# A joined three-stage kernel: rotary embedding by swapped partitions, and six layers' inverse roots taken by a power on GpSimd

## The reference

```python
# stage A: layernorm + scale/shift, self-attention, cross-attention, gated feed-forward (16 heads of 64)
# stage B:
def _rope(x, theta):                       # pairs (even, odd) of a head's 64 dimensions are turned
    x1, x2 = (x[..., 0::2], x[..., 1::2])
    return concatenate([x1 * cos - x2 * sin, x1 * sin + x2 * cos], axis=-1)
xn = _rmsnorm(x, gamma1)
q, k = _rope(xn @ q_w + q_b), _rope(xn @ k_w + k_b)
attn = softmax(where(causal, q @ k.T / 8, -inf))          # 16 heads of 64
...                                                       # 31 routed experts, top 3
# stage C: six layers, each with three norms
def _ln(x, eps=1e-05):
    m = mean(x); v = var(x)
    return (x - m) * rsqrt(v + eps)
x = x + self_attention(_ln(x) ...); x = x + cross_attention(_ln(x) ...); x = x + feed_forward(_ln(x) ...)
# behind it a last stage of 64 experts
```

## Time and profile before

| what | us |
|---|---|
| median of 3 runs (lowest, highest) | 2443.45 (2440.22, 2444.05) |
| the profiled execution, its own time | 2436.98 |
| its span in the profile | 2435.4 |
| PE busy | 2093.1 (86%) |
| DVE busy | 1613.7 (66%) |
| ACT busy | 1247.7 (51%) |
| POOL busy | 140.8 (6%) |
| stage A's self-attention | about 18 to 300 |
| stage B's self-attention | about 454 to 709 |
| the layers of stage C | about 780 to 2263 |

### The profile page before, as it was taken

How to read it: one execution, slowest core, us unless ns; L and a number is a source line. 1 busy time by engine, 2 the same in 40 slices (tenths; PEclk the granted TensorE clock), 3 DMA queues, 4 the chain that set the end, 5 groups by cost and what they waited for, 6 DMA issues and landing times.

```text
span 2435.4 us, 32516 instructions
## 1 busy us (share of the span) xinstructions
PE 2093.1 (86%) x11008; PEld 917.6 (38%) x11008; DVE 1613.7 (66%) x4148; ACT 1247.7 (51%) x2398; POOL 140.8 (6%) x130
## 2 busy tenths in 40 slices
PE   7999988899999988778878887988788788868998
PEld 3444455545556522322232223322232322233433
DVE  6766576666757787467746756684677467653564
ACT  4565544355543346646645663666366546635311
POOL 0000000111120200000000000000000000010000
PEclk9999999899999989979997997999799979989999
DMA  4000000300010100001000100010010001030000
GB/s 156 1 1 1 1 1 1 122 1 1 1 55 3 46 1 27 1 27 45 1 25 3 46 1 27 3 44 1 27 45 2 5 23 27 5 104 1 1 1 9
DMA packets 38037, 54.36 MB, mean 22 GB/s; under 512 B 5073, under 2 KB 34546, under 8 KB 36338
## 3 DMA queue, kind: packets, MB, share of 16 engines
q1 hardware_dynamic: 37874, 52.28, 6.8%
HBM read 32.34 MB, written 0.52 MB: 13 GB/s over the span
## 4 chain that ended last, share of the span: by engine, by line
PE 40%; DVE 10%; ACT 9%; issue 4%; SPq 1%; DMA 0%; ACTq 0%; POOL 0%; DVEq 0%; POOLq 0%
PE ps L1938 7%; PE ps L1918 5%; ACT big L2418 4%; PE ps L1899 4%; DVE C_nm L2595 4%; PE ps L2066 3%; PE ps L1983 3%; PE ps L2173 2%; PE ps L2078 2%; ACT big L2498 2%; PE ps L2169 2%; PE ps L2194 2%; PE ps L2085 2%; PE ps L2094 2%; PE ps L2043 1%
## 5 line engine op out<-in xcount | busy, mean ns | idle before, releaser
L2595 DVE TENSOR_REDUCE C_nm<-ps 128x1 f32<-128x512 f32 x768 | 501.4, 685 | 178.0 <-PE ps L1899 173.7
L2418 ACT ACTIVATE big<-ps 128x512 f32<-128x512 f32 x768 | 427.9, 595 | 226.7 <-PE ps L1918 216.0
L1899 PE MATMUL ps<-C_attn 62*128 62x512 bf16 x768 | 274.5, 415 | 60.8 <-DVE C_nm L2595 51.6
L1918 PE MATMUL ps<-C_attn 64*128 64x512 bf16 x768 | 251.3, 393 | 63.2 <-ACT big L2418 52.7
L1938 PE MATMUL ps<-big,C_attn 128*32 128x512 f32 x1536 | 210.6, 621 | 13.3 <-ACT big L2418 13.3
L1899 PEld LDWEIGHTS ps<-C_attn 62*128 62x128 bf16 x768 | 63.1, 94 | 302.3 <-DVE C_nm L2595 165.9
L1918 PEld LDWEIGHTS ps<-C_attn 64*128 64x128 bf16 x768 | 59.3, 93 | 272.7 <-ACT big L2418 205.2
L2498 ACT ACTIVATE big<-ps,C_biasx 77x512 f32<-77x512 f32 x192 | 115.6, 679 | 57.8 <-PE ps L2070 57.7
L790 DVE TENSOR_REDUCE A_nm<-ps 128x2 f32<-128x1024 f32 x64 | 78.4, 1225 | 58.8 <-PE ps L618 58.5
L2557 ACT ACTIVATE big<-ps 128x512 f32<-128x512 f32 (+1 forms) x66 | 39.4, 597 | 149.0 <-PE ps L2169 146.7
L717 ACT ACTIVATE A_pT<-ps 128x512 f32<-128x512 f32 x128 | 69.9, 599 | 77.1 <-PE ps L634 77.1
(11 more groups left out here) (364 smaller groups left out, 3733.4 us busy)
## 6 DMA issues: line engine op xcount, KB each, us to landing
C_attn<-C_first SPq DMA_DIRECT2D x144, 128.0 KB, 2.4
C_w<-in_C_w SPq DMA_DIRECT2D x6, 1090.0 KB, 5.0
C_attn<-in_D_ew SPq DMA_DIRECT2D x4, 1536.0 KB, 10.5
big<-in_B_ew SPq DMA_DIRECT2D x8, 514.0 KB
normw_later<-in_norm_w SPq DMA_DIRECT2D x1, 2304.0 KB, 16.4
A_w<-in_A_w SPq DMA_DIRECT2D x2, 1024.0 KB, 11.8
A_w<-in_A_w SPq DMA_DIRECT2D x2, 768.0 KB, 8.8
B_w<-in_B_w SPq DMA_DIRECT2D x1, 1536.0 KB, 10.1
```

The costliest lines, as they stand in the source:

```text
L1899: pe.matmul(ps[:, bank, :], lhsT=qs[side(hp, MAX_ROW), b, 2 * q + pq, t * P:(t + 1) * P], rhs=ks[side(hp, MAX_ROW), b, 2 * q + pq, :], sta ...
L1918: pe.matmul(ps[:, bank, :], lhsT=ks[side(1 - hp, HALF), b, 2 * q + pq, kt * P:(kt + 1) * P], rhs=qs[side(1 - hp, HALF), b, 2 * q + pq, :], ...
L2418: act.activation(prob[:, kt % 2, pq, 1 - hp, :], ps[:, bank, :], ACT.Exp, scale=SCALE)\
L2595: dve.tensor_reduce(nm[:, q % 2, t, pq, hp:hp + 1], ps[:, bank, :], AX.X, ALU.max, negate=True).then_inc(emptied[bank], 1)
```

## The change

Three things change. (1) In stage B the swapped projections "qr" and "kr" are no longer computed. The weights stay in the reference's order of dimensions. ACT copies q and k with their bias from PSUM into `B_rot[:, i, 0]`; SP swaps neighbouring partitions by two DMAs of 64 rows of 2 KB into `B_rot[:, i, 1]`; DVE multiplies the first by cos into `B_q` or `B_k`; POOL multiplies the second by sin, and then adds it to DVE's product. (2) In `self_attention_block`, for stages A and B both, `add_out` moves ahead of the step's other work on DVE. (3) In stage C the twelve-instruction root leaves DVE. At the same slots POOL adds eps and raises to the power -0.5; DVE's APPLY waits for it.

```diff
-    pieces = ("q", "qr", "k", "kr") if causal else ("q", "k")
-    column = {"q": WQ, "qr": WQR, "k": WK, "kr": WKR}
-    at_step = (("q", "qr"), ("k", "kr"), ("v",), ()) if causal else (("q",), ("k",), ("v",), ())
+    column = {"q": WQ, "k": WK}
...
@@ POOL, stage B
-                            pool.wait_ge(roped, n * 4 + 2 * i + 2)
-                            if n >= 3:
-                                pool.wait_ge(s_done, (n - 2) * TB)
-                            pool.tensor_tensor(dst[:, n % 3, :], rot[:, i, 0, :], rot[:, i, 1, :], ALU.add)\
+                            turned_rows = rot[:, i, 1, :]
+                            pool.wait_ge(swapped[i], 32 * (n + 1))
+                            pool.tensor_tensor(turned_rows, turned_rows, rope[i][1], ALU.mult).then_inc(sin_done, 1)
+                            pool.wait_ge(sin_done, 2 * n + i + 1)
+                            pool.wait_ge(cos_done, 2 * n + i + 1)
+                            pool.tensor_tensor(dst[:, n % 3, :], dst[:, n % 3, :], turned_rows, ALU.add)\
                                 .then_inc(ready, 1)
+        if rope is not None:
+            @block.sync
+            def _(sp):
+                for n in range(N):
+                    for i, ready in enumerate((q_ready, k_ready)):
+                        sp.wait_ge(raw_ready, 2 * n + i + 1)
+                        if n:
+                            sp.wait_ge(ready, n)
+                        for r in range(2):
+                            sp.dma_start(rot[r:P:2, i, 1, :], rot[1 - r:P:2, i, 0, :]).then_inc(swapped[i], 16)
@@ ACT
+            def copy_raw(n, i):
+                bank = arrived(act, ("qk"[i], n))
+                if n:
+                    act.wait_ge(swapped[i], 32 * n)
+                    act.wait_ge(cos_done, 2 * n + i - 1)
+                act.activation(rot[:, i, 0, :], ps[:, bank, :], ACT.Identity,
+                               bias=bias[:, n % PAIRS, BIAS_Q + i:BIAS_Q + i + 1]).then_inc(emptied[bank], 1)
+                drained(act, ("qk"[i], n))
+                act.sem_inc(raw_ready, 1)
...
+                if rope is not None and t in (1, 2) and n + 2 < N:
+                    copy_raw(n + 2, t - 1)
                 copy_turned(i)
@@ DVE
-            def rotate(n, i, r):
-                bank = arrived(dve, (pieces[2 * i + r], n))
...
-                dve.scalar_tensor_tensor(rot[:, i, r, :], ps[:, bank, :], bias[:, n % PAIRS, 2 * i + r:2 * i + r + 1],
-                                         rope[i][r], ALU.add, ALU.mult).then_inc(emptied[bank], 1)
+            def rotate(n, i):
+                dve.wait_ge(raw_ready, 2 * n + i + 1)
+                if n >= 3:
+                    dve.wait_ge(s_done, (n - 2) * TB)
+                dve.tensor_tensor((qT, kT)[i][:, n % 3, :], rot[:, i, 0, :], rope[i][0], ALU.mult).then_inc(cos_done, 1)
...
+                if t == 0 and n >= 3:
+                    add_out(n - 3)
...
                 if i + 2 < STEPS:
                     row_max(i + 2)
                 if i + 1 < STEPS:
                     weights(i + 1)
-                if t == 0 and n >= 3:
-                    add_out(n - 3)
...
@@ stage C
+for places, of in zip(GPSIMD, VECTOR):
+    for i in "123":
+        places["ROOT" + i] = of.pop("SEED" + i)
...
+                pool.memset(power[:], -0.5).then_inc(power_set, 1)
...
+                    for i in range(3):
+                        if s in at[("ROOT1", "ROOT2", "ROOT3")[i]]:
+                            pool.wait_ge(spread_known, norms(n, i))
+                            pool.tensor_scalar(m.lnv[:, 0:TB], m.mv[:, 0:TB, 1], EPS, None, ALU.add).then_inc(with_eps, 1)
+                            pool.wait_ge(with_eps, norms(n, i))
+                            pool.tensor_tensor(m.rs[:, 0:TB], m.lnv[:, 0:TB], power[:], ALU.pow).then_inc(rooted, 1)
...
-                def seed():
-                    rstd_steps(c_, dve, m, TB, False)
...
                 def apply(n, count):
+                    dve.wait_ge(rooted, count)
```

More of the change, by code:

```diff
@@ L28 @@
 RSQRT_MAGIC = 0x5F3759DF
-BIAS_V = 4
+BIAS_Q, BIAS_K, BIAS_V = range(3)
 R_BO1, R_BO2, R_FB2, R_OB, R_G1, R_G2, R_F2B = range(7)
@@ L508, in self_attention_block @@
     filled, emptied, place = ring.filled, ring.emptied, {}
-    WQ, WK, WV, WO, WQR, WKR = (P * i for i in range(6))
+    WQ, WK, WV, WO = (P * i for i in range(4))
     N = B * PAIRS
@@ L661, in _ @@
                 opening.tensor(pe, ps[:, S_BANK, :])
-            for what in pieces:
+            for what in "qk":
                 project(0, what)
@@ L675, in _ @@
                     weigh(n - 1, t)
-                if n + 2 < N:
-                    for what in at_step[t]:
-                        project(n + 2, what)
+                if n + 2 < N and t < 3:
+                    project(n + 2, "qkv"[t])
                 if t == TB - 1 and n >= 2:
@@ L733, in _ @@
                 opening.scalar(act, ps[:, S_BANK, :])
+            if rope is not None:
+                copy_raw(0, 0)
+                copy_raw(0, 1)
             exps(0)
@@ L737, in _ @@
             copy_v(1)
+            if rope is not None:
+                copy_raw(1, 0)
+                copy_raw(1, 1)
             for i in range(STEPS):
@@ L808, in add_out @@
                     .then_inc(emptied[bank], 1)
-            for what in pieces:
-                take(0, what)
+            for i in range(2):
+                take(0, i)
             row_max(0)
@@ L814, in _ @@
             weights(0)
-            for what in pieces:
-                take(1, what)
+            for i in range(2):
+                take(1, i)
             for i in range(STEPS):
                 n, t = divmod(i, TB)
+                if t == 0 and n >= 3:
+                    add_out(n - 3)
+                    if n - 3 == PAIRS - 1 and tail is not None:
+                        drained(dve, ("out", PAIRS - 1))
                 if n + 2 < N and t in (1, 2):
-                    for what in at_step[t - 1]:
-                        take(n + 2, what)
+                    take(n + 2, t - 1)
                 if i + 2 < STEPS:
@@ L825, in _ @@
                     weights(i + 1)
-                if t == 0 and n >= 3:
-                    add_out(n - 3)
-                    if n - 3 == PAIRS - 1 and tail is not None:
-                        drained(dve, ("out", PAIRS - 1))
                 if opening is not None:
@@ L1838, in stage_c @@
         d_w_loaded = (d_w_loaded0, d_w_loaded1)
-        y_added = m.sem("C_y_added")
+        y_added, spread_known, with_eps, rooted = \
+            (m.sem("C_" + s) for s in ("y_added", "spread_known", "with_eps", "rooted"))
         rt = Router(m, "C_router", e_b, first, 1)
@@ L2577, in stats @@
                         ins = dve.bn_aggr(m.mv[:, t, :], m.st[:, t, :])
-                        c_.after(ins) if t == TB - 1 else c_.step(ins)
-                def seed():
-                    rstd_steps(c_, dve, m, TB, False)
+                        if t < TB - 1:
+                            c_.step(ins)
+                    ins.then_inc(spread_known, 1)
                 def apply(n, count):
+                    dve.wait_ge(rooted, count)
                     for t in range(TB):
@@ L2984, in lay_out @@
     out["A_w2"] = i[a + "ff_w2"].reshape(4, P, P).transpose(1, 0, 2)
[L2987 to L2989 removed]
     q, k, v, o = (i[f + x] for x in ("q_w", "k_w", "v_w", "o_w"))
[L2991 to L2997 removed]
+    out["B_bias"] = stack([i[f + x] for x in ("q_b", "k_b", "v_b")], 1).reshape(PAIRS, P, 3).transpose(1, 0, 2)
+    out["B_w"] = pairs(o, q, k, v)
+    sign = np.tile(np.array([-1.0, 1.0], np.float32), DH)
+    out["theta"] = stack([np.tile(np.repeat(i[f + "theta"], 2), 2), sign], 1)
     out["positions"] = np.arange(S, dtype=np.float32)
```

37 lines of the change are left out of this document (10 added, 27 removed).

## The result

| what | before | changed |
|---|---|---|
| median of 4 runs each, on one chip, us | 2443.75 | **2411.23** |
| lowest, highest | 2440.22, 2451.71 | 2408.69, 2417.96 |
| the profiled execution, its span | 2435.4 | 2411.0 |

The ratio is 0.9867, with a 95% interval of 0.9835 to 0.9899: 32.5 us faster, where the forecast was 46. A later comparison, with six runs of the changed kernel, gave 0.9892 (0.9870 to 0.9914); over all runs of either kernel the medians are 2442.9 (44 runs) and 2414.8 (10 runs), 28 us. The two profiled executions lie 24 apart.

A forecast was written before the change was run, and what follows sets the result against it. PE, busy 86% of the span, was taken as the bound. Terms -12 - 32 + 11 + 3.6 - 10 - 7 = -46 us gave 2391 for the profiled execution, 2397 for the median (-1.9%); range 2368 to 2426.

The forecast's parts named there:

- Part 1, -12: Stages A and B: moving the residual sum ahead removes PE's 12.9 us of ring waits; -12 us, ends -8 and -13.
- Part 2, the projections, -32: Stage B: PE loses two projections of four a pair, 2.3 us in each of 14 pairs; -32 us.
- half of 1.99, twice: Stage B: two projections take 1.99 us, so each dropped one saves half; with a 0.34 us wait, 2.3 a pair.
- The collisions, +11: Stage B: POOL's instructions delay DVE's scaling or the product ahead, so PE waits 0.8 us in each of 14 pairs; +11.
- The opening, +3.6: Start of stage B: k's longer chain delays first scores 2 to 3 us, the second pair another 1; +3.6, ends 1 and 6.
- Part 3, -10 and -7: Stage C, root on POOL: six exposed roots gain 1.7 us each, -10; 30 others shorten waits for maxima by 0.25 each, -7.
- the upper bound of 1.8: Stage C: POOL's root if a power costs as much as its 512-element product, 1.27 us; 0.7 was taken.
- do not fall below 51.6: Stage C: sign that the forecast is wrong, PE's waits for row maxima not falling below their 51.6 us.
- Rival 5: Stage C: the roots bring nothing since PE was waiting for ACT there; -29 us, 2414; chance 0.09.
- Rival 2, the clock: Stage C: a shorter pause avoids PE's first clock fall, about 3 us six times; -16 more, 2381; chance 0.13.
- Rival 3, a slow power: Stage C: slow power delays DVE's maxima; A and B's gain gone at about 4 us a root, 2494 at 6; chance 0.07.
- Rival 4: Stage B: the swap lands late, over 7 us, each us beyond costing PE 14; 2447 at 11 us; chance 0.04.

The follow-up runs named there:

- the sum alone: Kernel before with only the sum into the residual moved ahead on DVE, stages A and B: 2420.82 us, ratio 0.9919.
- no projections and no GpSimd: Changed kernel with the rotary step's sine product and sum on VectorE instead of GpSimd, all pairs: 2408.74 us, again 2413.31.
- The added third instruction: Changed kernel with one more GpSimd product, never read, for each q and k in stage B: 2435.38 us, ratio 0.9964.
- the kernel with a root of 4.7: Changed kernel with each GpSimd power in stage C done four times in a row: 2454.20 us, ratio 1.0055.
- The roots alone: Kernel before with only stage C's roots moved to GpSimd: 2448.26 us, ratio 1.0019.
- everything but the roots: Changed kernel with stage C's roots back on VectorE: 2415.70 us, ratio 0.9888; in more rounds 2413.97, 0.9885.

## Why the prediction was right, and where its terms were off

**Direction and size.** Faster was forecast at 0.89, and 2411 lies inside the range, 14 above the forecast. Terms went wrong in both directions, and part of the closeness is luck: stages A and B were forecast at 29 us and gave 26 in the profiles, with errors that cancel, and stage C was forecast at 17 and gave nothing. The forecast's miss is stage C's.

**Part 1, -12: right in its place, somewhat low.** No wait for the sum is left, and stage A's attention is 13.9 us shorter. Moved alone, the call won 22: the 0.34 us a pair in stage B that the prediction counted under part 2 belong here (5 us in stage B), and what is left, some 3 us, is within what runs differ by.

**Part 2, the projections, -32: over-sized.** The step that failed is "half of 1.99, twice". Two projections in a row start the next piece of work 1.91 us on, one alone 1.06 (504.22 to 505.28): the second costs 0.86. Two kernels confirm it: from the sum alone (14.80) to no projections and no GpSimd (13.09 in two pairs) a pair loses 1.71, twice 0.86. Two of them and the 0.34 are 2.06, of which a pair won 1.93.

**The collisions, +11: right kind, wrong place.** In the eight clean pairs they cost at most 0.13 each, not 0.8 (13.22 against 13.09 to 13.22 with GpSimd out of the way). But of the two pairs in which DVE also works at the next norm, the first lost 1.5 to them and 0.7 to the clock. The added third instruction shows how near the edge is: 1.0 us a pair more. The Trainium skill (SBUF — State Buffer, "Who interferes with whom") has the two block each other for the whole instruction, and by that rule the length of DVE's own instruction should not matter; the product of four elements that took 1.23 us bears it out.

**The opening, +3.6: too low, and the largest error in stage B.** The first scores came 2.75 us later (2 to 3 forecast). But the stretch up to the first mark holds three of the 14 pairs as well, for which the prediction booked 3 x (2.3 - 0.8) of gain, so that by its own terms the stretch should have been 0.9 us shorter. It was 4.6 longer: the opening cost about 9 us in these terms. PE's pauses grew by 9.8, since POOL had the second and the third pair's work back to back (462.65 to 474.48) and stretched the scalings beside it: with GpSimd out, 3.5 us of it are gone. The rest is the chain of copy, swap and product that nothing hides there, and the clock: 4.6 us behind the first scores and 3.5 later ran at half of it, an estimated 4 us, half of these 8.1.

**Stage B in all** went from 254.8 to 241.2: -13.6, where part 2's terms were -17.4. Behind the opening it won 18.2, where 11 pairs at 1.5 were forecast, 16.5: the over-sized projections and the over-sized collisions cancelled.

**Part 3, -10 and -7: wrong.** Two steps failed, the price and the worth of the freed time. The price: the root was taken as 0.7 us, nearer to the small copy; it took 1.47 of waiting, 1.04 of it the power, near the upper bound of 1.8. So the exposed pauses shrank by 0.95, not 1.7, and at five places: the sixth, which the prediction took for one of 5.71 us though it was 2.63, grew by 1.1. That leaves 3.6 us in PE's list of waits. And the freed time of DVE: the waits for maxima went from 51.6 to 51.1, with 0.9 between the means of all profiles, instead of 7. The prediction's own sign ("do not fall below 51.6") was missed by that margin alone. That a maximum of the other unit covers POOL's root does not hold at 10 of the 30 places, where DVE waits 1.47 us as at the exposed ones. That PE is held at the maxima by the chain of its own scores, and not by DVE being busy with a root, is argued from this and not shown by itself. Rival 5 (2414, "the roots bring nothing") is the nearest to what happened, though PE was not waiting for ACT: the exposed pauses did shorten, and the gain is below what runs differ by.

**Rival 2, the clock:** the fall behind the pause did not go away (0.50 in the six us behind 1236.2, against 0.54), nor did the second (0.50 from 1259 to 1274); the pause shrank by less than forecast. **Rival 3, a slow power:** it did not come about, but its turning point of about 4 us fits the kernel with a root of 4.7, 0.55% slower than before. **Rival 4:** the swap landed in 2.0 us (at most 4.1) and was hidden in all pairs but the first ones.

**Still open:** whether roots on POOL themselves lower the clock. The roots alone had a mean clock of 0.933 over ten runs, against 0.936 for the kernel before over 40, and everything but the roots also had 0.931. Behind stage B the profiles have 0.915 with roots on POOL (eight) and 0.920 with roots on DVE (four), but with the new rotary step in place 0.916 either way (two profiles each). Nothing run here separates the cause from where the work happens to fall.

## What to carry to other kernels

Before pricing an engine's work by its total, ask which single instruction the critical engine waits for, and whether the added work can meet that one: GpSimd busy 5.6 us of a pair cost at most 0.13, at 8.2 us 1.0 more. Work freed on an engine that was not what the wait was for gives next to nothing, even 60 us of it; and one instruction earlier in another engine's queue can be worth more than projections taken away: moved alone, the sum gave 22 us, and everything else that the change does in stage B another 8 (249.6 to 241.2). Where a change opens pauses, the clock behind them belongs in the sum: in stage B it went from 0.99 to 0.95. Where the clock moves a kernel by 10 us from run to run, compare the length of the stage that was changed, and the waits in it.

## What the runs showed of the hardware

- GpSimd's power on 128 partitions: 0.58 us for one column, 1.01 to 1.04 for four.
- A VectorE instruction of four elements with two inputs in SBUF can take 1.13 to 1.23 us beside a GpSimd sum or product of 512; a row maximum out of PSUM at the same place kept its 1.21 (465.84, beside POOL's product at 465.33).
- GpSimd busy in SBUF can stretch a VectorE scaling too: two of 128x384 from 0.75 to 2.77 us, four of 128x128 from 1.10 to 2.21.
- The same program's granted clock falls on different matmuls from one execution to the next; a mean clock lower by 0.006 went with 9.4 us.
